# A two-layer vision tower on one core: the order of the second pass rewritten, gathers one direction ahead, a norm centred by matmul

## What is computed

```python
h = h + ssm(norm(h))            # layer 0: 4 small MLPs of each token give A, B, C and delta;
                                # state = (delta*state + (1-delta)*u*B*dt) * exp(A*dt); y = sum(state*C) + u*D
h = h + experts(norm(h))        # 8 experts 192->768->192 with gelu, the best 2 of each token
h = h + mamba_both(norm(h))     # layer 1: x @ down (96 wide); a Mamba block forwards and one backwards
                                # (4 taps, silu, 16 states, gate), each with a layer norm; sum @ up
h = h + mixture(norm(h))        # 8 linear experts 192->192, softmax router, the best 2 of each token
```

## Time and profile before

| | |
|---|---|
| median of 3 runs | 996.31 us (991.14 to 999.53) |
| the profiled execution | 992.72 us, its span 990.9 us |
| TensorE busy | 754.4 us (76%) |
| VectorE | 576.4 us (58%) |
| ScalarE | 405.6 us (41%) |
| GpSimd | 396.0 us (40%) |
| mean granted TensorE clock | 0.872 of full speed |
| DMA | 179.51 MB, mean 181 GB/s |

### The profile page before, as it was taken

The page is one execution under the profiler, slowest core; times in us unless marked ns, Lnnn a source line. Parts: engine busy times, 40 slices in busy tenths (PEclk is TensorE's granted clock), DMA queues, the critical chain, the costliest instruction groups (busy, mean ns, idle before and its releaser), DMA issues.

```text
span 990.9 us, 11474 instructions
## 1 busy us (share of the span) xinstructions
PE 754.4 (76%) x3588; PEld 593.2 (60%) x3588; DVE 576.4 (58%) x975; ACT 405.6 (41%) x880; POOL 396.0 (40%) x311
## 2 busy tenths in 40 slices
PE   7878788784648799888897587858678678965846
PEld 5646556463438698778895355646466456653624
DVE  4177869778844414112115797788957886589120
ACT  2557282580323244223454545545343551643010
POOL 1156646844842322230002543454365326444403
PEclk9989798895867899999999778889799888987867
DMA  9569545543773688897757686947594649486011
GB/s 343 153 237 354 171 119 140 153 121 90 207 216 98 178 246 249 258 259 245 227 175 177 170 214 160 235 128 198 158 240 130 170 142 261 108 218 185 17 49 46
DMA packets 84668, 179.51 MB, mean 181 GB/s; under 512 B 12740, under 2 KB 32832, under 8 KB 83840
## 3 DMA queue, kind: packets, MB, share of 16 engines
q1 hardware_dynamic: 79776, 171.55, 60.5%
q0 software_dynamic: 4832, 7.24, 2.4%
...
## 4 chain that ended last, share of the span: by engine, by line
PE 27%; DVE 12%; DMA 8%; issue 8%; ACT 4%; SPq 4%; POOL 2%; DVEq 0%; POOLq 0%; ACTq 0%
PE PS L1633 26%; DMA BB<-rows_d 5%; DVE ST L1298 3%; DMA xp<-slots_d 3%; DVE PS L1287 2%; POOL PR L778 1%; ACT dA L952 1%; SPq L497 1%; POOL WX L786 1%; ACT L902 1%; DVE p_OM L1351 0%; PE PS L1844 0%; SPq L608 0%; DVE m_Xr L1166 0%; DVE m_ACC L1531 0%
## 5 line engine op out<-in xcount | busy, mean ns | idle before, releaser
L1633 PE MATMUL PS<-PR,CM 128*128 128x304 f32 (+1 forms) x672 | 188.0, 423 | 58.1 <-POOL PR L778 47.5
L778 POOL TENSOR_TENSOR PR<-ST,V 128x608 f32<-128x608 f32 x96 | 142.2, 1481 | 196.5 <-DVE ST L1298 132.9
L1633 PEld LDWEIGHTS PS<-PR,CM 128*128 128x128 f32 x672 | 131.4, 230 | 100.6 <-POOL PR L778 62.2
L952 ACT ACTIVATE dA<-dA,negA 128x304 f32<-128x304 f32 x192 | 94.0, 541 | 158.7 <-DMA BB<-rows_d 158.4
L1298 DVE TENSOR_TENSOR_SCAN ST<-dA,PS 128x608 f32<-128x608 f32 x96 | 136.3, 1420 | 27.5 <-ACT dA L952 16.3
L1004 ACT ACTIVATE HID<-PS,WX 128x128 f32<-128x128 f32 x204 | 59.5, 368 | 137.5 <-PE PS L1633 137.3
L691 POOL TENSOR_TENSOR dA<-dA,aP 128x607 f32<-128x607 f32 x48 | 71.1, 1483 | 79.1 <-ACT aP L972 75.9
L1287 DVE TENSOR_TENSOR PS<-BB,PS 128x608 f32<-128x608 f32 x96 | 76.0, 792 | 21.8 <-DMA BB<-rows_d 16.8
L1492 DVE TENSOR_TENSOR xp<-PS,WXB 128x192 f32<-128x192 f32 x34 | 12.2, 358 | 123.4 <-PE PS L1633 123.4
L1633 PE MATMUL PS<-XT,WX 128*128 128x128 f32 x408 | 82.1, 284 | 1.1 <-ACT HID L1004 1.0
L1633 PE MATMUL PS<-XT,WXR 128*128 128x128 f32 x408 | 81.5, 283 | 0.0
...
## 6 DMA issues: line engine op xcount, KB each, us to landing
...
```

What stands on the lines that cost most here:

```text
L778: nc.gpsimd.tensor_tensor(PRq[:, c % 2], STq[:, c % 2], DIRS[k].Cw.unsqueeze(1).broadcast_to([128, QB, T]), ALU.mult).then_inc(q_product.s ...
L952: last = nc.scalar.activation(dAq[:, slot, i, :], dAq[:, slot, i, :], ACT.Exp, scale=negA[:, j:j + 1])
L1633: return nc.tensor.matmul(out, lhsT, rhs, start=first, stop=last)
```

## The change

- *TensorE, second pass*: at each n `sum_step` comes first, before all other pieces. `direction_out` is at n = 1 (was 2), `direction_var` at 2 (3 and 5). The z projection and taps of direction 0 stand at n = 1 and 2 of part B (was 4); those of direction 1 at n = 7, 8 and 9 of part B (was n = 0 of part A). The mixture's six parts are at n = 1 to 6 of part A, its rest in three parts at n = 9 to 11, in another PSUM bank (`REST_BANK`, the one of direction 1's sums), which the up projection's rest uses too; the first sum of direction 1 waits until `final` of g - 2.
- *TensorE, first pass*: `first_sum` of n - 1 comes first for n = 1 to 10, before variance, mean, hidden layers, patches and the others.
- *The norm of the next group* isn't centred on VectorE. `expert_centre` multiplies the residual by the matrices CENT (identity less 1/192) and NEG (-1/192), four matmuls; ScalarE squares the result from PSUM. The down weights are centred once in `fold_biases`, so `project_down` takes the residual itself, and one multiplication by the reciprocal root (`scale_down`, 96 rows) replaces the scaling of all 192. The residual lies in two sets of buffers in turn (`RES`), so ScalarE's copy of it (L1086, L1087) goes. ScalarE now copies the rest of the finished group to its output buffer (`rest_copied`), where VectorE adds the mixture.
- *Gathers*: `find_rows`, `gather` and `combine` are done for the group after the next, `far`, in part B (n = 3, 4 to 6, and 9). Group 1's go through GA0, which lies in the ring of the BB rows, so SP waits for `combine(1)` before it reads the first rows.
- *SP*: `write_rows(g, 1)` after the last read of direction 0, `write_gates` after the last read of direction 1, `store` and `store_end` in direction 1.
- *VectorE*: `steps(g, 1)` at n = 7 (was 6), the residual of the output at n = 8, `add_mixture` at n = 7 (was 5), `add_mixture_rest` at n = 0 of part B (was n = 7 of part A), the scalings at n = 0 (was 2), `gates_top` at 3 (4), `gates_rows` at 7 (6).
- *ScalarE*: follows these places; each root is taken by itself (`output_root` at n = 3), `inputs(nxt, 0)` at n = 3 of part B (was 4), `inputs(g, 1)` stays at n = 2 of part A. The centred squares and the root for `tail` are at n = 11 of part A, the root for `nxt` at n = 0 of part B.

The diff, cut; in order SP, GpSimd, ScalarE (the new function), VectorE (new functions, `part_a`, `part_b`), TensorE (`sum_step`, the first pass, new functions, `part_a`, `part_b`).

```diff
+            sp.wait_ge(mixed.sem, mixed.after(1, TILES))
             for g in range(GROUPS):
                 rows_there(g, 0)
                 for c in range(QSTEPS):
-                    if c == QSTEPS - 1:
-                        write_rows(g, 1)
                     read_rows(g, 0, c)
-                    if c == 10 and g >= 2:
-                        store(g - 2)
+                write_rows(g, 1)
...
                 for c in range(QSTEPS):
-                    if c == QSTEPS - 1 and g:
-                        write_gates(g - 1)
                     read_rows(g, 1, c)
...
+                    if c == 4 and g + 2 < GROUPS:
+                        load_next(g + 1)
+                    if c == 8 and g >= 2:
+                        store(g - 2)
+                    if c == QSTEPS - 1 and g >= 2:
+                        store_end(g - 2)
+                if g:
+                    write_gates(g - 1)
                 if g + 1 < GROUPS:
                     write_rows(g + 1, 0)
...
-                        gate_inputs(mix, n + QSTEPS - MIX_FROM)
+                    if mix is not None and n < MIX_PARTS:
+                        gate_inputs(mix, n)
                     if nxt == 0 and n in IN_PART_A:
...
             def part_b(g, tail, nxt):
...
-                    if tail is not None and n >= MIX_FROM:
-                        gate_inputs(tail, n - MIX_FROM)
+                    if far == PER_HALF and n == 4:
+                        rows_stored(every)
+                    if far is not None and n == 4:
+                        pool.wait_ge(rows_ready.sem, rows_ready.after(far, 1))
+                        pool.sem_inc(turn_taken, 1)
+                    if far is not None and n in (4, 5, 6):
+                        gather(far, (n - 4,))
...
+            def centred_squares(g):
+
+                act.wait_ge(l_centred.sem, l_centred.after(g, 1))
+                nc.scalar.activation(L.SQm, PS[:, L_BANK, 0:T], ACT.Square).then_inc(L.ln_squares.sem, 1)
+                nc.scalar.activation(L.SQr, PS[0:DR, X_BANK, 0:T], ACT.Square).then_inc(L.ln_squares.sem, 1)
...
+            def scale_down(g):
+                dve.wait_ge(L.ln_rstd.sem, L.ln_rstd.after(g, 1))
+                dve.wait_ge(l_down.sem, l_down.after(g, 1))
+                nc.vector.tensor_tensor(BOTT, PS[0:BN, X_BANK, 0:T], L.RS[0:BN, :], ALU.mult).then_inc(L.ln_x.sem, 1)
...
+                dve.wait_ge(up_bias_mm, 1)
+                nc.vector.tensor_tensor(cm("up_b"), cm("up_b"), PS[:, Q_BANK, 0:2], ALU.add)
+                nc.vector.tensor_tensor(cm("down"), cm("down"), PS[:, Q_BANK, 8:8 + BN], ALU.subtract)
+                nc.vector.tensor_tensor(cr("down")[0:DR, :], cr("down")[0:DR, :], PS[0:DR, Q_BANK, 8:8 + BN], ALU.subtract).then_inc(up_bias_ready, 1)
...
-                    if mix is not None and n == 5:
+                    if nxt == 0 and n == 2:
+                        find_rows(nxt)
+                    if nxt == 0 and n == 7:
+                        combine(nxt)
+                    if n == 7 and mix is not None:
                         add_mixture(mix)
-                    if mix is not None and n == 7:
-                        add_mixture_rest(mix)
-                    if g is not None and n == 6:
+                    if n == 7 and g is not None:
                         if tail is not None:
                             dve.wait_ge(out_mm.sem, out_mm.after(tail, 2))
                         steps(g, 1)
...
-                        if n == 6:
+                        if n == 5:
                             output_norm(tail, 1)
...
+                        if n == 8:
+                            if mix is not None:
+                                dve.wait_ge(rest_copied.sem, rest_copied.after(mix, 1))
+                            output_residual(tail)
+                    if n == 9:
+                        if nxt is not None:
+                            expert_residual(nxt)
+                        if tail is not None:
                             centre(Q, Q, tail, 0, Q_BANK)
...
+                    if n == 11 and mix is not None and tail is None:
+                        add_mixture_rest(mix)
...
             def part_b(g, tail, nxt):
+                mix, far = before_tail(tail), after_next(nxt)
                 for n in range(QSTEPS):
                     if g is not None:
                         direction_step(g, 1, n)
...
+                    if n == 0:
+                        if nxt is not None:
+                            scale_down(nxt)
+                        if tail is not None:
                             scale(Q, tail, 0)
-                        if n == 4:
+                        if mix is not None:
+                            add_mixture_rest(mix)
+                    if n == 1 and g is not None:
+                        gated_output(g, 0)
+                    if n == 3:
...
+                        if far is not None:
+                            find_rows(far)
...
+                        if g is not None:
+                            output_norm(g, 0)
...
+                        if tail is not None:
                             gates_rows(Q, tail, Q_BANK)
-                    if n == 7:
...
                             steps(nxt, 0)
-                        if g is not None:
-                            output_norm(g, 0)
+                    if n == 9 and far is not None:
+                        combine(far)
...
+                if c == 0 and k == 1 and g >= 2:
+                    pe.wait_ge(final.sem, final.after(g - 2, 1))
...
+                    if s is not None and 0 < n < QSTEPS - 1:
+                        first_sum(s, n - 1)
                     if n == 1:
                         if p is not None:
                             variance(P, p, 0, MEAN_BANK)
...
-                    if s is not None and n:
+                    if s is not None and n == QSTEPS - 1:
                         first_sum(s, n - 1)
...
+            def expert_centre(g):
+
+                h = RES[g % 2]
+                pe.wait_ge(M.residual.sem, M.residual.after(g, 1))
+                mm(PS[:, L_BANK, 0:T], CENT[:, :], h.Hm, True, False)
+                mm(PS[:, L_BANK, 0:T], NEG[:, :], h.HrK, False, True)
+                mm(PS[:, X_BANK, 0:T], NEG[:, :], h.Hm, True, False)
+                mm(PS[:, X_BANK, 0:T], CENT[:, :], h.HrK, False, True).then_inc(l_centred.sem, 1)
...
+            def project_down(g):
+
+                h = RES[g % 2]
+                mm(PS[0:BN, X_BANK, 0:T], cm("down"), h.Hm, True, False)
+                mm(PS[0:BN, X_BANK, 0:T], cr("down"), h.HrK, False, True).then_inc(l_down.sem, 1)
...
             def part_a(g, tail, nxt, mix):
                 for n in range(QSTEPS):
-                    if n == 0:
-                        if g is not None:
-                            pe.wait_ge(dt_raw.sem, dt_raw.after(g, 1))
-                            project_z(1).then_inc(in_mm.sem, 1)
-                        if tail is not None:
-                            sum_step(tail, 1, QSTEPS - 1)
-                        if g is not None:
-                            pe.wait_ge(c_copied.sem, c_copied.after(g, 1))
-                            project_taps(1).then_inc(in_mm.sem, 1)
+                    if n == 0 and tail is not None:
+                        sum_step(tail, 1, QSTEPS - 1)
+                    if g is not None and n:
+                        sum_step(g, 0, n - 1)
                     if tail is not None:
+                        if n == 1:
+                            direction_out(tail, 1)
                         if n == 2:
-                            direction_out(tail, 1)
-                        if n == 3:
                             direction_var(tail, 1)
...
-                        if n == 3:
+                        if n == 4:
                             project_states(g, 1)
-                        if n == 4:
+                        if n == 5:
                             project_steps(g, 1)
...
+                    if mix is not None and 0 < n <= MIX_PARTS:
+                        mixture(mix, n - 1)
+                    if n == 7 and tail is not None:
+                        if mix is not None:
+                            pe.wait_ge(main_mixed.sem, main_mixed.after(mix, 1))
+                        pe.wait_ge(bn_done.sem, bn_done.after(tail, 2))
+                        for k in range(2):
+                            mm(PS[:, Q_BANK, 0:T], UPW[:, k, 0:DM], YS[:, k, :], k == 0, k == 1)
+                        for k in range(2):
+                            last = mm(PS[:, REST_BANK, 0:T], UPW[:, k, DM:], YS[:, k, :], k == 0, k == 1)
+                        last.then_inc(up_proj.sem, 1)
+                    if n == 8:
+                        if nxt is not None:
                             if g is not None:
...
-                    if g is not None and n:
-                        sum_step(g, 0, n - 1)
```

(43 more changed lines are left out.)

291 lines of the change are left out of this document (118 added, 173 removed).

## The result

The change makes the kernel faster: **960.23 us** median of 4 runs (958.99 to 965.53), 993.72 before (4 runs, 987.0 to 999.53), a ratio of 0.9675 with a 95% interval of 0.96 to 0.9751. A second set of runs of the same kernel gave 0.973 (0.970 to 0.976). Forecast were 984.3 us and a range down to 970: right in sign, less than half in size, and outside the range. The profiled execution of after took 961.01 us, its span 959.2.

The account below looks back on a forecast made before the run. It took the second pass to be bound by waits in VectorE's stream. Groups and tail -25, expert blocks' end +7 and first pass +6 make -12 from 996.3: 984.3 us, range 970 to 1004.

Parts of the forecast that it names:

- first pass: First pass: scaling some 3.5 us later delays all hidden layers, +2 in each of three bodies, +6 us, bounds 0 and +10.
- third group: Second pass, third group: changed waits and work, summed over a step-by-step walk, make it 6.0 us shorter.
- fourth group: Second pass, fourth group: no next group, thus no turn, no steps and no combine; -2.5 us.
- first group: Second pass, first group: loses find, combine and gathers, gains a wait for its own centring; -3.5 us.
- second: Second pass, second group: without mixture and rest, its wait at `scale_down` is about 4.5 instead of 7.7; -7.5 us.
- tail: Tail: the mixture's rest matmuls stand behind the up projection, residual near 934; -5.5 us, bounds -2 and -9.
- end of the expert blocks: End of the expert blocks: z projection, taps and centring cost 4 us, `combine(1)` before the row reads 3; +7 us.
- the turn to the next group: Turn to the next group: length unchanged, but `combine` moves to n = 9 of part B and fills the wait; -2.8 us.
- norm: Next group's norm: VectorE loses 4.4 us of wait and 2.1 of work; the new `scale_down` chain adds 7.7.
- The rule that I left out: VectorE's steps: gate products moved away from the shared port lock could give up to 1.8 us a group; not counted.
- TensorE, held by its sums: Rival, chance 0.15: small matmuls behind sums waiting for GpSimd's product run at a lower clock; slower, 1006 us.
- The losses stay hidden: Rival, chance 0.2: first pass makes up its delay and only combine is lost at the expert blocks' end; 974 us.

Follow-up runs that it names:

- after, again: The kernel after the change, unaltered, timed again on one of the chips used for the follow-up runs: 964.74 us against 991.25, ratio 0.973.
- experiment 1: First pass's sums put first in the kernel before: 1.0029; that one edit undone in the kernel after: 0.9719.
- combine at 7: Kernel after, with find, gathers and combine back in the first direction of the group before, combine at n = 7: 0.9926.
- experiment 3: Kernel after, gathers a direction ahead undone, in two runs: combine at n = 7 of the first direction 0.9926, at n = 8 0.9845.
- experiment 5: Kernel after with two needless GpSimd products added in each direction: behind the product of n = 7 0.994, behind that of n = 9 0.9788.
- before with the sums first: Kernel before with one edit: in the second pass TensorE issues the sum of step n-1 at the head of step n: 1.0133.
- experiment 2: Second pass: kernel after with sums and the mixture's parts last again, 0.9861; kernel before with sums first alone, 1.0133.
- experiment 6: Kernel after with GpSimd's gate products, the mixture's parts and the gates' write two steps earlier, as before the change: 0.9701.
- the earlier combine: Kernel after with group 1's rows combined at n = 8, ahead of the last expert block's copy: 957.16 us, ratio 0.9688.

## Why the prediction was wrong

Three steps failed: the first pass's delay was priced as time of the whole (+6, where the runs show nothing that can be told from 0), the third group was given a combine in part B that isn't there, and the fourth group's sum had no term for the small waits and lengthened operations that went (-2.5, measured -8.1). Forecast of each term, against the table:

| term | forecast | after | after, again |
|---|---|---|---|
| first group | -3.5 | -3.2 | -3.4 |
| second | -7.5 | -7.9 | -6.5 |
| third | -6.0 | **-10.0** | **-11.2** |
| fourth | -2.5 | **-8.1** | **-8.2** |
| tail | -5.5 | -6.9 | -7.1 |
| end of the expert blocks | +7 | +6.0 | +3.3 |
| first pass | +6 | **-3.2** | **+0.6** |

With 1.6 us (2.1) by which the first scan of all came later, these make the -31.7 (-30.5) between the spans. Most of the missing 20 us are in three terms.

*First pass, the failed step.* "The scaling follows some 3.5 us later" came true (3.8). "All of the hidden layers hang on it" was wrong as a price: by the router's scaling, 17 us later in the same group, the delay is gone. That scaling lies 24.0 to 26.2 us behind the group's first scan in the three traces with the old order, 24.8 to 26.6 in those of after, its repeat and experiment 1. The sum of the step before no longer stands ahead of the router's variance; I had named this return and not sized it. By experiment 1 the term isn't told from 0 (+2.9 us, -0.7 to +6.5); the 3.2 us of the trace are within what pass 1 varies. That lies in the bounds of 0 to +10 that I gave, at their end.

*Third group: who does the work.* The waits were close. Decays -0.6 forecast, -1.2 measured; mixture -2.7 and -2.4; the mean's 4.4 gone as said; `scale_down` with the rest 6.1 against 6.4 with 1.3 for the rows of direction 1, which did not come; logits -0.9 and -0.9; small waits -0.9 and -0.9. The failed step is *the turn to the next group*: that `combine` "is moved from part A to n = 9 of part B, ahead of the last scans, and fills the wait: -2.8". In this group no combine stands in part B, for the fourth group has no next: `combine(3)` and its `find_rows` had already run in the second. The turn kept its length (write at 797.84, first product at 812.70, 14.9 us as in the earlier trace rows) and its wait (5.6 for 5.4), but 3.0 us of combine and 1.3 of find left the group's work. I had also written that the first group loses these; it doesn't. Second, the *norm* cost 3.1 us of VectorE before, not 2.1, one scaling having taken 1.73 us, and 0.5 after. Third, the operation of 2.46 us took 0.63. These durations make 8.7 us; busy time, which counts overlapping operations once, fell by 7.1.

*The turn where the combine does stand.* In the second group it is at n = 9, 3.05 us long, and the wait that it was to fill is still 5.7 us (5.4 before):

```profile
698.80 0.33 SPq L621 DMA_DIRECT2D rows_d<-q_DL  x1
716.53 0.80 DVE L1293 TENSOR_TENSOR PS<-BB,PS 128x608 f32<-128x608 f32 x1 [5.67 <-DMA BB<-rows_d]
```

The combine did cover some of it: without one there (combine at 7, experiment 3) VectorE waits 7.8 us. But "None of this moves" failed: the turn took 17.7 us (17.1 in the repeat), not 14.9. What stands in it is the read of the gates, three DMAs issued ahead of the rows. The last landed 12.0 us after the first was issued, before the change 9.4, and the product started 2.3 to 2.4 us behind that landing in both. Why the gates took longer there isn't shown. In the third group they took 9.3.

*First and second group: right by luck.* The second's waits fell by 6.6 us, above all two for which my walk had 0.9 at most (3.4 for GpSimd's product, 2.4 for the residual, both gone), not by a filled turn. The first kept the combine that I took out of it.

*Fourth group: mis-sized by what its waits depend on.* I let only the mixture and a little of the decays fall. VectorE's listed waits fell from 15.6 to 9.9 us: 7.5 went from four of them (3.0 for the sums of a finished direction, 1.5 for a product, 1.1 for the residual, 1.9 of the mixture's) and 2.8 came for the mixture's rest; and three operations that had taken 1.79, 1.73 and, among the gates, 1.26 us took 0.63, 0.46 and 0.37, 3.3 us together. Putting the sums and the mixture's parts last cost this group 4.9 us, 2.8 of them work of VectorE, so that the places on TensorE, for which my walk has under 1 us, are more than half of it.

*The rule that I left out.* I wrote that the port pair that VectorE and GpSimd share, an exclusive lock by the Trainium skill (SBUF — State Buffer, "SBUF: two separate sides"), could give back up to 1.8 us a group, and took none. The sum of lengthened VectorE instructions, formed as in experiment 5, is 21.0 us before and 12.8 after: by group 4.7, 6.0, 5.6, 4.6 against 4.1, 5.0, 2.6, 1.1. These 8.2 us less of work, 3.0 and 3.5 in the third and fourth group, aren't 8.2 us of gain for sure: in before with the sums first the sum fell as far, to 13.8, and the kernel was 13 us slower, since its waits grew by more. My reason for leaving it out, that the scan's own product runs beside the steps anyway, was wrong in the third and fourth group, where VectorE reached the operation of the earlier trace rows 0.3 us after that product had ended, since it waited for the mixture first. Experiment 5 agrees with the rule as to the mechanism, 13.7 us more of such time for two more products. That the gain here is what the order on TensorE happened to give agrees with experiment 2: with sums and mixture last the sum is 16.1 us again, 4.2 of it in the fourth group, while experiment 6, which moved GpSimd's gate products, left it at 13.4 (12.4 in the repeat of after).

*End of the expert blocks:* +6.0 for +7, of other parts: the last copy 4.7 us later, counted from the first pass's last scan, instead of 4, the turn 1.4 instead of 3. The single number is partly chance (+3.3 in the repeat), but the term holds over the table: 215.7 us is the mean of the seven rows with this end as in after, 208.9 of the three with that of before.

*Tail:* the residual came 8.1 us earlier against the last scan, where a value near 934 meant 9.3; -6.9 remained, as the parts between the residual and the end took 1.2 us from it, not the 3.8 that I let them.

*The rivals.* "TensorE, held by its sums" is what before with the sums first shows, 13 us slower; in the kernel after, with clocks of 0.86 to 0.93, it doesn't occur, since the chains had moved too. I gave it 0.15 as a rival of the whole and missed that the order works for the change once the rest has moved: undoing it, with the mixture's place, costs 13 us. "The losses stay hidden", 974, was nearest, for another reason: only one of its two losses did.

**What stays open:** which of the moved chains makes the sums pay, and how much of the 13 us is the mixture's place (none was moved alone); why the gates' read is longer in the second group, and what the turns would take with the rows read ahead of the gates, which no run tried; whether the earlier combine is faster than after, 0.9688 against 0.973 with intervals that overlap; and why pass 1 and the expert blocks vary by several us between runs of the same code.
